# Attention scores in two 64-row products for pairs of tiles, with constant products, an earlier context and earlier shared experts

## What is computed

```python
x = x + tanh(g_xattn[l]) * xattn_l(layernorm(x), ctx)
x = x + tanh(g_ffn[l]) * ffn_l(layernorm(x))
# xattn: softmax(q @ k.T * scale) @ v over the 32 keys of the batch, by head
# ffn: sum over the picked experts of weight * expert(x), plus shared experts (l = 0, 2)
```

## Time and profile before

| | us |
|---|---|
| three runs: median (lowest to highest) | 698.18 (695.52 to 699.17) |
| the profiled execution | 695.84 |
| its span, first to last instruction | 694.0 |
| PE busy in it | 590.9 |
| DVE busy | 406.1 |
| ACT busy | 293.6 |
| POOL busy | 293.4 |
| mean granted clock of TensorE | 0.927 |

### The profile page before, as it was taken

One profiled execution on the slowest core, in us unless ns is written; L12 is line 12 of the kernel. 1 busy time (PEld: TensorE's weight loads), 2 busy tenths in 40 slices (PEclk: granted clock), 3 DMA queues, 4 the chain that ended last, 5 costly groups with the idle time before them and its releaser, 6 DMA issues.

```text
span 694.0 us, 13651 instructions
## 1 busy us (share of the span) xinstructions
PE 590.9 (85%) x3946; PEld 455.4 (66%) x3946; DVE 406.1 (59%) x1637; ACT 293.6 (42%) x732; POOL 293.4 (42%) x354
## 2 busy tenths in 40 slices
PE   5788879799947889989995889888899998898991
PEld 3366755599923667659993456654799855655991
DVE  3665764588856767342224886745588676653443
ACT  3446524144415554324441555442344345433660
POOL 3111477366631015477552201467266611272551
PEclk9979999999979988599998999999999999779996
DMA  8990011323255000022224100012233140012214
GB/s 260 230 418 31 17 39 43 82 78 89 76 158 216 1 0 32 17 72 71 75 58 130 42 1 2 24 43 84 58 89 90 44 122 1 0 50 79 61 50 129
DMA packets 56200, 54.88 MB, mean 79 GB/s; under 512 B 8216, under 2 KB 50992, under 8 KB 55072
## 3 DMA queue, kind: packets, MB, share of 16 engines
q1 hardware_dynamic: 48288, 39.75, 19.8%
q0 software_dynamic: 7840, 14.25, 6.3%
HBM read 34.99 MB, written 20.86 MB: 80 GB/s over the span
## 4 chain that ended last, share of the span: by engine, by line
PE 55%; DVE 10%; issue 10%; POOL 8%; ACT 6%; DMA 5%; DVEq 4%; SPq 1%; POOLq 0%; ACTq 0%
PE bank L894 16%; PE bank L906 11%; POOL slots L570 6%; PE bank L727 5%; PE bank L711 4%; ACT pay L989 2%; DVE x L1569 2%; PE bank L613 2%; PE bank L882 2%; PE bank L849 2%; PE bank L672 2%; PE bank L851 2%; PE bank L685 2%; PE bank L866 2%; DVE stat L1159 2%
## 5 line engine op out<-in xcount | busy, mean ns | idle before, releaser
L600 POOL DMA_INDIRECT result<-xn,row x133 | 131.3, 987 | 111.2 <-DVE row L1519 98.7
L570 POOL DMA_INDIRECT slots<-pay,pos x112 | 110.9, 990 | 60.9 <-issue 32.8
L533 POOL TENSOR_TENSOR rstd<-spread,minus_half 128x4 f32<-128x4 f32 (+1 forms) x33 | 34.2, 1036 | 211.0 <-DVE spread L1152 178.6
L894 PE MATMUL bank<-xnT,gat 128*128 128x128 f32 x808 | 109.9, 280 | 1.1 <-DVE gat L1528 1.1
L906 PE MATMUL bank<-w,hsh 128*128 (+1 forms) x752 | 106.3, 276 | 2.9 <-DVE hsh L1535 1.1
L894 PEld LDWEIGHTS bank<-xnT,gat 128*128 128x128 f32 x808 | 99.4, 194 | 2.4 <-ACT xnT L1082 1.3
L906 PEld LDWEIGHTS bank<-w,hsh 128*128 128x128 f32 x752 | 94.8, 192 | 4.0 <-issue 3.0
L613 PE MATMUL bank<-onesb 128*128 128x512 bf16 x224 | 68.3, 444 | 16.2 <-DMA pay<-result 16.2
L727 PEld LDWEIGHTS bank<-vblk,probT 128*128 128x128 f32 x384 | 51.2, 201 | 38.0 <-issue 25.1
L727 PE MATMUL bank<-vblk,probT 128*128 128x36 f32 x384 | 51.6, 282 | 13.7 <-ACT probT L1029 10.6
L1546 DVE COPY xn<-bank 128x128 f32<-128x128 f32 x110 | 31.4, 286 | 50.0 <-PE bank L906 40.3
(11 more groups left out here) (233 smaller groups left out, 1033.0 us busy)
## 6 DMA issues: line engine op xcount, KB each, us to landing
xg<-slots SPq DMA_DIRECT2D x133, 64.5 KB
w<-in_w SPq DMA_DIRECT2D x4, 2048.0 KB, 11.9
pay<-result SPq DMA_DIRECT2D x21, 256.0 KB, 4.4
w<-in_w SPq DMA_DIRECT2D x1, 2560.0 KB, 19.3
w<-in_w SPq DMA_DIRECT2D x1, 2304.0 KB, 14.3
result<-xn,row POOLq DMA_INDIRECT x133
slots<-zeros SPq DMA_DIRECT2D x2, 1032.0 KB, 24.3
slots<-pay,pos POOLq DMA_INDIRECT x112, 2.4
```

The source lines that it names most:

```text
L570: pool.indirect_dma_start(out=(slots1[k] if l == 1 else slots)[:, :], out_offset=bass.IndirectOffsetOnAxis(ap=pos[:, t, k:k + 1], axis=0), ...
L600: pool.indirect_dma_start(out=result[:, :], out_offset=bass.IndirectOffsetOnAxis(ap=row[:, s % TURN:s % TURN + 1], axis=0), in_=ysb[:, s % ...
L894: last = pe.matmul(bank[2 + p][:, c * P:(c + 1) * P], weights[:, c * P:(c + 1) * P], xgT[:, p, :], start=True, stop=True)
```

## The change

Scores: banks 2 and 3 become one tensor `two`. A tile's scores are two products of 64 rows and 256 columns, for heads 0 to 7 and 8 to 15, one into each bank; an even tile takes the first 256 columns of both banks, an odd one the last. PE computes them for two tiles at once, in odd steps, behind the values, and signals once per pair; it waits until DVE has subtracted all tiles before the pair. In layer 2 the mask is two products of 256 columns. DVE's step is split in three functions whose order alternates between odd and even steps, each with a drain of its own.

Constant products: one or three are put ahead of the values of almost every tile of layers 0 to 2, and other counts change.

Layer 3's keys and values move from step 20 of layer 2 to the tail of layer 1 as `last_context`, with banks 4 and 5 and a buffer `kT3` of their own. The shared parts of layer 2 stand at steps 17 to 20 and 24 to 28 (`PART_AT`); those of layer 0 stay. In layer 2, ACT's exp of the picked logits moves from step 23 to behind the shared parts, with a load of the Silu table after it.

```diff
+        bank = [banks(0), banks(1)]
+        two = banks(2, 2)
+        bank += [two[:, 0:512], two[:, 512:1024]] + [banks(i) for i in range(4, 8)]
+        def scores(n):
+            return two[:].rearrange("p (r o) -> p r o", r=2)[:, :, n % 2 * 256:(n % 2 + 1) * 256]
...
-                   logits=10, pick=11, ranks=12, scatter=12, place=13, next_context=20),
+                   logits=10, pick=11, ranks=12, scatter=12, place=13),
...
-        BUSY_VALUES = [{15: 6}, {14: 2, 15: 3}, {13: 2, 14: 2, 15: 2}]
-        BUSY_TOKENS = [{}, {}, {}, {0: 1, 1: 1, 2: 1, 3: 1}]
-        BUSY_QUERIES = [{}, {}, {}, {0: 2, 1: 2, 2: 2, 3: 2}]
+        BUSY_VALUES = [{**{n: 1 + n % 2 * 2 for n in range(2, 15)}, 15: 8}, {**{n: 1 + n % 2 * 2 for n in range(0, 13)}, 13: 3, 14: 3, 15: 4},
+                       {**{n: 1 + n % 2 * 2 for n in range(0, 13)}, 13: 2, 14: 2, 15: 2}]
+        BUSY_TOKENS = [{}, {0: 3}, {}, {0: 1, 1: 3, 2: 2, 3: 2}]
+        BUSY_QUERIES = [{}, {0: 8}, {}, {0: 2, 1: 2, 2: 2, 3: 2}]
+        BUSY_SCORES3 = {0: 4, 1: 1, 2: 1, 3: 1}
-        BUSY_ROUTED = [{}, {2: 3, 3: 3}, {2: 2, 3: 3}, {0: 2, 1: 2, 2: 2, 3: 3}]
-        BUSY_LOGITS = [{2: 14}, {2: 5, 3: 6}, {2: 2, 3: 6}, {0: 1, 1: 2, 2: 5, 3: 6}]
-        BUSY_RANKS = [{}, {2: 5, 3: 10}, {2: 3}, {2: 4, 3: 12}]
-        BUSY_BEFORE_LOOP = [8, 22, 0, 24]
-        BUSY_AT_FIRST = 0
+        BUSY_ROUTED = [{}, {2: 3, 3: 3}, {2: 2}, {0: 2, 1: 2, 2: 2, 3: 3}]
+        BUSY_LOGITS = [{2: 14}, {2: 6, 3: 6}, {}, {0: 1, 1: 2, 2: 5, 3: 6}]
+        BUSY_RANKS = [{}, {2: 5, 3: 12}, {}, {0: 2, 1: 2, 2: 4, 3: 20}]
+        BUSY_BEFORE_LOOP = [16, 14, 14, 24]
+        BUSY_AT_FIRST = 8
-        FIRST_PART = [20, 0, 24, 0]
+        PART_AT = [list(range(20, 32)), [], [17, 18, 19, 20, 24, 24, 25, 26, 27, 28], []]
...
+            def last_context():
+                pe.wait_ge(Z["c_kT"], 3)
+                pe.matmul(bank[4][:, 0:P], WK[3], ctxT[:], start=True, stop=True).then_inc(Z["c_k"], 1)
+                for b in range(B):
+                    pe.matmul(bank[5][0:KEYS, b * P:(b + 1) * P], ctxT[:, b * KEYS:(b + 1) * KEYS], WV[3],
+                              start=True, stop=False)
...
-                    if N >= 2:
-                        pe.wait_ge(Z["a_sub"], N - 1)
...
-                    last = pe.matmul(out, qT[:, g % 2, n % GT * P:(n % GT + 1) * P],
-                                     kblk[:, g].rearrange("p h k -> p (h k)"), start=True, stop=l != 2)
...
+                if s % 2 and 0 <= s + 1 < NTILE:
+                    n0, g = s + 1, (s + 1) // GT
+                    pe.wait_ge(Z["a_qT"], g_at(l, g) + 1)
...
+                    pe.wait_ge(Z["a_sub"], n_at(l, n0))
...
+                    half = HEADS // 2
+                    for n in (n0, n0 + 1):
+                        for r in range(2):
+                            dims = slice(r * P // 2, (r + 1) * P // 2)
+                            last = pe.matmul(scores(n)[:, r], qT[dims, g % 2, n % GT * P:(n % GT + 1) * P],
+                                             kblk[dims, g, r * half:(r + 1) * half].rearrange("p h k -> p (h k)"),
+                                             start=True, stop=l != 2)
+                        if l == 2:
+                            for r in range(2):
+                                last = pe.matmul(scores(n)[:, r], maskT[:, n * P:(n + 1) * P],
+                                                 every[:, 0:half].rearrange("k h i -> k (h i)"), start=False, stop=True)
+                    last.then_inc(Z["a_s"], 1)
...
                 if l == 1:
                     next_context(l, 0)
+                    last_context()
...
                 rest_of_parts(l, shared)
+                if l == 2:
+                    exp_logits(l)
+                    preload(ACT.Silu)
...
+                if s % 2:
+                    soft(l, s)
+                    norm(l, s - 2)
+                    residual(l, s - 4)
+                else:
+                    norm(l, s - 2)
+                    residual(l, s - 4)
+                    soft(l, s)
```

More of the change, by code:

```diff
@@ L185, in flamingo, with banks @@
         unused = sb("unused", [P, 1])
[L188 removed]
+        def banks(i, n=1):
+            return ctx.enter_context(nc.psum_tensor(f"bank{i}", [P, n * 512], F32))
+        bank = [banks(0), banks(1)]
[3 more added lines that the diff above has]
+            return two[:].rearrange("p (r o) -> p r o", r=2)[:, :, n % 2 * 256:(n % 2 + 1) * 256]
         slots = nc.dram_tensor("slots", [E * REGION, ROW], F32, kind="Internal").ap()
```

168 lines of the change are left out of this document (80 added, 88 removed).

## The result

| | before | after |
|---|---|---|
| median of the runs, us (lowest to highest) | 698.67 (695.52 to 701.09) | 734.15 (731.17 to 736.10) |
| profiled execution, us | 695.84 | 736.10 |
| its span | 694.0 | 733.1 |
| mean granted clock in it | 0.927 | 0.894 |

The change makes the kernel slower by 5.2%: the ratio is 1.0521, with an interval from 1.0481 to 1.0561. Forecast were 689.5 us, and at most 705. The span grew by 39.1 us.

The account below looks back on a forecast made before the run. PE was taken to bound attention steps, partly at half clock, with GpSimd's scatters pacing layers 0 and 2. Terms 2.4 - 0.9 - 5.2 - 0.6 - 1.0 - 1.0 = -6.3 took 695.84 to 689.5 us, range 672 to 705.

Parts of the forecast that it names:

- I take the half clock as gone, since the constant products fill the waits: First scores to first scatter, layers 0 to 2: no half clock left; stretches 58.4, 54.0, 55.4 us, sum +2.4.
- one rival for the clock: Rival: full clock returns in half of its places, 698.6 us, chance 0.18; none at all gives 708.
- The chain: Attention, layers 0 to 2: one chain per pair of tiles, 6.2, 6.1 and 6.8 us at full clock.
- Halves at once: A pair's scores: passes on different array halves run beside each other, eight in five turns, 1.08 us.
- halves in series: Rival: second half's passes wait for the first's, +15.4, 705 us; chance 0.18 shared with no clock regained.
- Changes of mode: Switching between 128, 64 and 32 rows: taken at nothing; bound two changes a pair of 0.1 each, +4.8.
- Tail of layer 1, -5.2: Group 1's to group 3's positions in layer 1: full clock brings 19.7 us to layer 2's 14.5.
- Tail of layer 2, -0.6: Before layer 2's loop: shared parts done earlier, so the loop waits for the scatters alone, -0.6 us.
- Start of layer 1, -0.9: Layer 1's first scores: constant products fill the queries' wait; scores take 1.08 + 0.1 in place of 2.07.
- Start of layer 0's loop, -1.0: Eight more products fit PE's 2.09 us wait; second tile's expert products go from 1.91 to 0.96 us.
- Layer 3, -1.0: Four products ahead of half-clock queries bring these from 2.07 to 1.04 us; the others taken as equal.
- covered work: Rival: the chain's waits cover work between the attention steps; 14 us go at 40%, 672 to 680, chance 0.22.

Follow-up runs that it names:

- pairs alone: Changed kernel with each score product over all 128 rows and without the constant products ahead of the values of most tiles: 757.05 us, ratio 1.0822.
- unpaired halves: Changed kernel with one tile's halves scored every step, VectorE always in even-step order, most per-step constant products dropped: three runs 746.91 to 762.63 us, a fourth (1950.93) left out.
- Full rows in series: Changed kernel with each score product over all 128 rows, so a pair's eight passes follow one another; constant products kept: 742.22 us, ratio 1.0600.
- The second execution of before: Kernel before the change, unchanged, profiled a second time: 695.28 us; the changed kernel, likewise unchanged and profiled again: 736.44 us.
- none: Changed kernel without constant products ahead of the values, except at each layer's last tiles: median 757.74 us, runs from 741.27 to 761.69.
- four and six: Changed kernel with four and six constant products ahead of the values in place of one and three: 725.47 us, ratio 1.0358.

## Why the prediction was wrong

**The step that failed: "I take the half clock as gone, since the constant products fill the waits."** The forecast gave the three stretches 58.4 + 54.0 + 55.4 = 167.8 us with none of it at half clock. They hold 65.2 us of it by PEclk, worth 32.6 (some 78, worth 39, with layer 0's start). The products were set against the clock of before, not against what the edit itself takes from it: pairs alone raised the half clock from 17.0 to 73.7 us, unpaired halves raised it too, by their single chain of scores or by what goes with it. I had one rival for the clock, and it began from before's half clock as the worst case (708). That the clock could fall in layer 2, where it was full, stood in no case; with it the range missed. Of the 45.4 us between the forecast's span (694.0 - 6.3 = 687.7) and 733.1 the three stretches make 25.7 (193.5 against 167.8), layer 2's tail 13.1 and layer 1's 3.6.

**The chain was sized fairly.** Plain pairs at full clock are 259.22 - 252.60 = 6.62 us in layer 1, where 6.1 were forecast, and 0.44 of them are transposes of another group put in between (from 258.78). The three stretches at full clock are 160.9 us against the 167.8, by an estimate that is low. The constants were put at 0.45 us a pair, 9.5 for 21 pairs; the table gives 160.9 - 152.8 = 8.1.

**Halves at once: right, its 1.08 partly by luck.** Eight passes take 1.07 us from their start to the next instruction (223.61 to 224.68), where 1.08 were taken as five turns. But two passes of different halves stand in 0.49 us together (237.78), so there are four turns, 4 x 0.215 = 0.86, and 0.2 around them. The fifth turn of the sum isn't there, and what is there the sum had taken at nothing. Full rows in series show 1.97 with the tail, near the upper bound of 1.72. The rival "halves in series" falls. Its price for the chain, 0.64 us for each of 21 pairs, 13.4, is about what full rows show: 177.6 - 160.9 = 16.7. The Trainium skill, TensorE: Matmul & The Clock Gate, Part 3, says that products on different row groups run at once, and this trace agrees. In pairs with the constant products the saving was worth more than its price in clock: full rows took 742.22 us where the halves took 734.15.

**Changes of mode: taken at nothing, and not nothing.** In layer 2 a pair's scores and masks take 407.69 - 405.72 = 1.97 us, where 1.08 + 0.62 = 1.70 were put. A tile's two masks take 0.32 (406.35 to 406.67), as forecast. But they part the two tiles' scores: a tile's four passes take 0.63 (405.72 to 406.35), two turns of 0.215 and 0.2 around them, so the 0.2 comes twice in a pair. That is 0.2 more, 1.4 us for seven pairs, within the bound; the rest of the difference stands where the clock falls, at 407.5. The Trainium skill, TensorEngine Tiling (Array Packing), Key Properties, says that a change of the tiling mode drains TensorE. The 0.2 around a block of passes may be such a change on either side; no run here tells it from other causes.

**Tail of layer 1, -5.2.** From group 1's to group 3's positions it took 308.5 - 293.1 = 15.4 us (14.5 forecast, 19.7 before), but group 1's came 14.6 us after the first scatter (293.1 - 278.5), 11.9 before, and the stretch to the loop only went from 41.0 to 39.4. The second execution of before had 35.67 without the change, that of the changed kernel 44.03. The term rested on a half clock that one execution had and the next hadn't.

**Tail of layer 2, -0.6.** It became +12.5, or +7.2 between the second executions. The sum held no clock for it, since it was full in the rows.

**Start of layer 1, -0.9: right in kind.** Scores at full clock take 1.07 us, and they are at full clock. But the next step now waits 1.63 us for the first exp (226.97), and the stretch is no shorter by it.

**Start of layer 0's loop, -1.0.** The 16 products end as the first tile is taken up at 144.94, 7.0 us after the last scatter, where 5.9 were forecast: they fill the wait and lengthen it by an us. From there to the same tile at its end the loop takes 54.96 us at full clock, before 56.63 at 0.97, so some 0.5 us remain of the 1.0. **Layer 3, -1.0:** the queries of group 1 came at full clock (1.13 us in place of 2.07), but with its two stretches at 55.6 us, against 55.0, nothing was gained.

**The rival "covered work" (672 to 680)** had 14 us go from the forecast's 167.8, to 153.8. By the estimate 6.9 went (160.9), by the one with layer 0's start some 13; as both are low, how much was covered stays open. The clock took more than it.

## What to carry to other kernels

An edit that makes a clock-gated engine's work shorter or lumpier has to be priced at both clocks: read the granted clock of each stretch, and ask what the edit takes out of the engine's stream before asking what constant work will put back. Constant products are no free cover: the 180 that stand between none and four and six in the three stretches, 39 us of them at 0.215, lengthened these by 21.9 us at full clock. Hold the clock column against the length of a known product: here it read 1.00 where products took twice their time. And a stretch whose clock differs between two executions of the same kernel carries no term of a sum: compare a second profile first.

## What was not expected of the hardware

- The same work at about the same busy share ran at either clock: layer 2's attention with TensorE busy for 92% at 1.00 before and at 0.77 after. The share hides two parts, 14% of waits at full clock and 1% at half.
- Half clock stayed while TensorE was busy for 20.05 of 20.50 us (407.5 to 428.0), and for 23.57 of 24.0 in the tail.
- The clock of a tail changed from one execution to the next: 0.79 and 1.00 in layer 1, 1.00 and 0.85 in layer 2 of the kernel before, with the same sum of the two, 92.3 and 92.2 us.
- Products on the two halves of the array run side by side even when four passes of one half stand ahead of the other's in the queue (1.14 us for eight, against 1.13).
